# Two ScalarE functions and one refinement in place of an integer guess with three: the reciprocal roots of a layer's results in a two-layer graph network

## What is computed

```python
def _layernorm(x, axis=-1, eps=1e-05):
    m = jnp.mean(x, axis=axis, keepdims=True)
    v = jnp.var(x, axis=axis, keepdims=True)
    return (x - m) / jnp.sqrt(v + eps)

h = jnp.maximum(_layernorm(x), 0.0)
# first layer: attention over each node's edges, 4 heads of 32
alpha = einsum(q[dst], k[src]) / sqrt(32)
ea = exp(alpha - segment_max(alpha, dst)[dst])
out = segment_sum(v[src] * ea / segment_sum(ea)[dst]) + h @ Wskip + bskip
x = x + out
h = jnp.maximum(_layernorm(x), 0.0)
# second layer: messages with edge features, scaled by in-degree, summed by node
x = x + second_layer(h, src, dst, edge_attr_64)
```

## Time and profile before

| | us |
|---|---|
| median of 3 runs | 1663.34 (1662.32 to 1664.62) |
| the profiled execution's own time | 1664.58 |
| its span, first to last instruction | 1662.8 |
| TensorE busy | 1470.4 (88%) |
| VectorE busy | 1347.6 (81%) |
| ScalarE busy | 1016.5 (61%) |
| GpSimd busy | 1083.1 (65%) |

### The profile page before, as it was taken

One profiled execution on the slowest core, in us unless ns is written; L12 is line 12 of the kernel. 1 busy time (PEld: TensorE's weight loads), 2 busy tenths in 40 slices (PEclk: granted clock), 3 DMA queues, 4 the chain that ended last, 5 costly groups with the idle time before them and its releaser, 6 DMA issues. The chain is left out here.

```text
span 1662.8 us, 34477 instructions
## 1 busy us (share of the span) xinstructions
PE 1470.4 (88%) x10545; PEld 1263.5 (76%) x10546; DVE 1347.6 (81%) x3688; ACT 1016.5 (61%) x2501; POOL 1083.1 (65%) x1202
## 2 busy tenths in 40 slices
PE   5888898699999999999999974899998999998996
PEld 4666777688888888888888863777776777777775
DVE  8879665299999999999999994677776777777675
ACT  5777888556555565656665513566665666665663
POOL 2554442577777777777777605777777777777772
PEclk9999999899999999999999996999999999999999
DMA  8899887556666666666666516677666767667672
GB/s 219 274 274 313 284 300 262 157 160 180 189 174 192 175 188 183 178 182 182 182 174 185 156 45 148 148 160 174 162 163 150 171 160 172 161 158 170 149 164 68
DMA packets 162552, 302.85 MB, mean 182 GB/s; under 512 B 104113, under 2 KB 107703, under 8 KB 157524
## 3 DMA queue, kind: packets, MB, share of 16 engines
q1 hardware_dynamic: 121503, 201.19, 41.9%
q0 software_dynamic: 40896, 99.90, 24.9%
HBM read 196.84 MB, written 104.12 MB: 181 GB/s over the span
## 5 line engine op out<-in xcount | busy, mean ns | idle before, releaser
L803 POOL DMA_INDIRECT sb_kv<-kv_rows,sb_src_all x500 | 492.9, 986 | 187.1 <-issue 131.3
L831 POOL DMA_INDIRECT sb_kv<-x_rows,sb_src_all x500 | 473.8, 948 | 209.3 <-issue 109.1
L1710 ACT ACTIVATE sb_hn<-sb_xn 100x128 f32<-100x128 f32 x500 | 240.5, 481 | 265.9 <-DMA sb_kv<-x_rows,sb_src_all 225.1
L1713 ACT ACTIVATE sb_vw<-sb_kv 128x128 f32<-128x128 f32 x500 | 239.6, 479 | 0.0
L1638 ACT ACTIVATE sb_hn<-sb_xn,sb_nstat 100x128 f32<-100x128 f32 x500 | 231.5, 495 | 0.0
L1400 DVE COPY sb_hT<-ps_b 128x400 f32<-128x400 f32 x250 | 142.2, 569 | 96.1 <-PE ps_b L2005 95.3
L1797 PE MATMUL ps_b<-sb_w,sb_memberT 128*125 128x256 f32 x800 | 201.6, 391 | 18.3 <-DVE sb_xn L921 9.2
L1660 ACT COPY sb_memberT<-ps_b 100x512 f32<-100x512 f32 x150 | 75.8, 506 | 205.7 <-PE ps_b L1885 205.7
L1797 PEld LDWEIGHTS ps_b<-sb_w,sb_memberT 128*125 128x125 f32 x800 | 146.2, 193 | 41.7 <-issue 14.7
L2005 PE MATMUL ps_b<-sb_member,sb_vw 128*128 128x100 f32 x1000 | 173.8, 278 | 0.0
L2005 PEld LDWEIGHTS ps_b<-sb_member,sb_vw 128*128 128x128 f32 x1000 | 157.4, 198 | 9.8 <-issue 9.8
(11 more groups left out here) (184 smaller groups left out, 3103.0 us busy)
## 6 DMA issues: line engine op xcount, KB each, us to landing
kv_rows<-sb_kv SPq DMA_DIRECT2D x26, 1120.0 KB
sb_xn<-x_rows SPq DMA_DIRECT2D x50, 507.8 KB
sb_xn<-in_x SPq DMA_DIRECT2D x50, 500.0 KB
out_rows<-sb_xo SPq DMA_DIRECT2D x49, 500.0 KB
x_rows<-sb_xo SPq DMA_DIRECT2D x24, 1015.6 KB
sb_kv<-in_edge_attr SPq DMA_DIRECT2D x500, 32.0 KB
sb_kv<-in_x SPq DMA_DIRECT2D x28, 560.0 KB
kv_rows<-sb_xn SPq DMA_DIRECT2D x13, 1120.0 KB
```

The lines of the kernel that those rows point to most:

```text
L803: pool.indirect_dma_start(out=kvs[:, k % 4, t, :], out_offset=None, in_=kv_rows, in_offset=bass.IndirectOffsetOnAxis(ap=src_all[:, n:n + 1 ...
L831: pool.indirect_dma_start(out=xs1[:, k % 4, t, :], out_offset=None, in_=x1, in_offset=bass.IndirectOffsetOnAxis(ap=src_all[:, n:n + 1], ax ...
L1710: nc.scalar.activation(hn1[:, t, :], xn1[:, k % 4, t, 0:D], ACT.Relu, scale=xn1[:, k % 4, t, D:D + 1], bias=xn1[:, k % 4, t, D + 1:XW]).th ...
L1713: nc.scalar.activation(hs1[:, t, :], xs1[:, k % 4, t, 0:D], ACT.Relu, scale=xs1[:, k % 4, t, D:D + 1], bias=xs1[:, k % 4, t, D + 1:XW]).th ...
```

## The change

In each of the 25 sets the integer guess and two of the three refinements go. The set on VectorE now has 7 steps and 10 instructions. Its first three steps give the variance, as before. Then ScalarE computes Ln of the variance and Exp of -0.5 times that (`roots`), which is 1/sqrt, each signalling; VectorE's step 3 waits for the second of them, and steps 3 to 5 refine the value once; step 6 is the shift. ScalarE does `roots` in the turn right after `exps(k - 1)`, and so ahead of `copy_q(k + 1, 0)`. On VectorE the remaining steps stand in other places: step 3, which waits, stands ahead of `soft_step` 5 (`tot_e`), step 4 ahead of `rtot`, step 5 ahead of `wr`, step 6 behind `wr`. The statistics of the table stage keep their three refinements.

```diff
@@ -42,6 +42,7 @@
 RSQRT_BITS = float(0x5F3759DF)
 NEWTON = 3
 STAT_STEPS = 4 + 3 * NEWTON + 1
+X1_STEPS = 7
 EARLY = 2
 POOL_STEPS = 6
 NEVER = 2.0 * TILES
@@ -209,6 +210,8 @@
         var = sb("var", [128, 2 * B])
         guess = sb("guess", [128, 2, 2 * B], I32)
         nwt = sb("nwt", [128, 2, 2 * B])
+        log_var = sb("log_var", [NODES, 2 * B])
+        root = sb("root", [NODES, 2 * B])
         nstat = sb("nstat", [NODES, TILES, 2])
         pstat = sb("pstat", [ROWS, PB * B, 2])
         pool_st = sb("pool_st", [ROWS, 6, 2 * B])
@@ -402,6 +405,7 @@
                 self.aT = s("alpha_turned")
                 self.soft = s("softmax_step")
                 self.exp = s("exp_done")
+                self.root = s("reciprocal_root_step")
                 self.wT = s("weights_turned")
                 self.vw = s("values_weighed")
                 self.agg = s("agg_ready")
@@ -599,7 +603,7 @@
                 sp.dma_start(segk[:, k % 2, :], rows).then_inc(A.seg[k % 2], 16)
 
             def store(m):
-                sp.wait_ge(A.stat, STAT_STEPS * (m + 1))
+                sp.wait_ge(A.stat, X1_STEPS * (m + 1))
                 rows = x1[2 * GROUP * m:2 * GROUP * (m + 1), :].rearrange("(s p t) c -> p s (t c)", s=2, t=B)
                 slots = slice(2 * (m % 2), 2 * (m % 2) + 2)
                 from_xo = xo[:, slots, :, :].rearrange("n s t c -> n s (t c)")
@@ -1260,7 +1264,7 @@
                 m = k // 2
                 dve.wait_ge(A.xo, 3 * k + g + 1)
                 if g == 0:
-                    wait(dve, A.stat, STAT_STEPS * (m - 2) + 1)
+                    wait(dve, A.stat, X1_STEPS * (m - 2) + 1)
                     if m < 2:
                         dve.wait_ge(P.pool_stat, POOL_STEPS * (PAIRS - EARLY))
                 for t in range(first, last):
@@ -1271,11 +1275,24 @@
             def x1_stat_step(m, n):
                 if n == 0:
                     dve.wait_ge(A.bn, 2 * (m + 1))
-                wait(dve, A.stat, STAT_STEPS * m + n)
+                if n == 3:
+                    dve.wait_ge(A.root, 2 * (m + 1))
+                else:
+                    wait(dve, A.stat, X1_STEPS * m + n)
                 both = xo[:, 2 * (m % 2):2 * (m % 2) + 2, :, :]
-                stat_math(n, st[0:NODES, m % 2, :, :], both[:, :, :, D].rearrange("n s t -> n (s t)"),
-                          both[:, :, :, D + 1].rearrange("n s t -> n (s t)"), slice(0, 2 * B), NODES
-                          ).then_inc(A.stat, 1)
+                rstd, shift = (both[:, :, :, D + i].rearrange("n s t -> n (s t)") for i in range(2))
+                square, part, v = nwt[0:NODES, 0, :], nwt[0:NODES, 1, :], var[0:NODES, :]
+                if n < 3:
+                    ins = stat_math(n, st[0:NODES, m % 2, :, :], rstd, shift, slice(0, 2 * B), NODES)
+                elif n == 3:
+                    ins = dve.tensor_tensor(square, root[:], root[:], ALU.mult)
+                elif n == 4:
+                    ins = dve.scalar_tensor_tensor(part, square, -0.5, v, ALU.mult, ALU.mult)
+                elif n == 5:
+                    ins = dve.scalar_tensor_tensor(rstd, part, 1.5, root[:], ALU.add, ALU.mult)
+                else:
+                    ins = stat_math(STAT_STEPS - 1, None, rstd, shift, slice(0, 2 * B), NODES)
+                ins.then_inc(A.stat, 1)
 
             def step0(k):
                 this, prev, nxt = real(k), real(k - 1), real(k + 1)
@@ -1298,37 +1315,30 @@
                 stats(2)
                 if prev:
                     soft_step(k - 1, 1)
+                if prev:
+                    soft_step(k - 1, 2)
+                if nxt:
+                    members(k + 1, 0)
+                if prev:
+                    soft_step(k - 1, 3)
+                if prev:
+                    soft_step(k - 1, 4)
                 stats(3)
                 if prev:
-                    soft_step(k - 1, 2)
+                    soft_step(k - 1, 5)
                 stats(4)
-                if nxt:
-                    members(k + 1, 0)
+                if prev:
+                    soft_step(k - 1, 6)
                 stats(5)
                 if prev:
-                    soft_step(k - 1, 3)
+                    soft_step(k - 1, 7)
                 stats(6)
-                if prev:
-                    soft_step(k - 1, 4)
-                stats(7)
-                if prev:
-                    soft_step(k - 1, 5)
-                stats(8)
-                if prev:
-                    soft_step(k - 1, 6)
-                stats(9)
-                if prev:
-                    soft_step(k - 1, 7)
-                stats(10)
                 if this:
                     scores(k, 2)
-                stats(11)
                 if prev:
                     weigh(k - 1)
-                stats(12)
                 if this:
                     head_sums(k)
-                stats(13)
                 if nxt:
                     members(k + 1, 1)
                 if prev:
@@ -1348,31 +1358,31 @@
 
                 scores(k, 0)
                 scores(k, 1)
+                stats(0)
+                stats(1)
+                stats(2)
                 for n in range(N_SOFT):
                     soft_step(k - 1, n)
                 scores(k, 2)
-                stats(0)
                 weigh(k - 1)
-                stats(1)
                 head_sums(k)
                 for n in range(N_SOFT):
-                    stats(n + 2)
+                    if n + 3 < X1_STEPS:
+                        stats(n + 3)
                     soft_step(k, n)
                 finish(k - 1, 0)
                 finish(k - 1, 1)
                 weigh(k)
                 finish(k - 1, 2)
-                for n in range(10, STAT_STEPS):
-                    stats(n)
-                    if n < 13:
-                        x1_stats(k - 1, n - 10)
+                for g in range(3):
+                    x1_stats(k - 1, g)
                 finish(k, 0)
                 finish(k, 1)
                 x1_stats(k, 0)
                 x1_stats(k, 1)
                 finish(k, 2)
                 x1_stats(k, 2)
-                for n in range(STAT_STEPS):
+                for n in range(X1_STEPS):
                     x1_stat_step(m, n)
 
             for k in range(-1, BATCHES - 1):
@@ -1665,6 +1675,12 @@
                 act.wait_ge(A.soft, N_SOFT * k + 3)
                 nc.scalar.activation(er[:], dl[:], ACT.Exp, scale=SCALE).then_inc(A.exp, 1)
 
+            def roots(m):
+                act.wait_ge(A.stat, X1_STEPS * m + 3)
+                nc.scalar.activation(log_var[:], var[0:NODES, :], ACT.Ln).then_inc(A.root, 1)
+                act.wait_ge(A.root, 2 * m + 1)
+                nc.scalar.activation(root[:], log_var[:], ACT.Exp, scale=-0.5).then_inc(A.root, 1)
+
             def relus(k, first, last):
                 for t in range(first, last):
                     if real(k):
@@ -1678,6 +1694,8 @@
                 relus(k + 2, 0, 1)
                 if real(k - 1):
                     exps(k - 1)
+                if k % 2 == 1 and 0 <= (k - 3) // 2 < BATCHES // 2:
+                    roots((k - 3) // 2)
                 if nxt:
                     copy_q(k + 1, 0)
                 relus(k + 2, 1, 3)
@@ -1699,6 +1717,7 @@
 
             for k in range(-2, BATCHES + 1):
                 step0(k)
+            roots(BATCHES // 2 - 1)
 
             def relu1(k, t):
                 if t == 0:
```

## The result

The changed kernel takes **1725.88 us** (median of 4 runs, 1723.76 to 1728.07), the kernel before 1663.98 beside it. The ratio is 1.0369, with a 95% interval of 1.0343 to 1.0394: 62 us slower. The forecast was 1705.5, in a range of 1688 to 1754.

What follows compares the result with a forecast made beforehand. VectorE was taken to bound the attention stage. A 2.22 us wait less 0.39 saved, times 23 turns, added 42.1 to 1664.58; less 1.2 for the profiled run gave 1705.5 us, own range 1691 to 1719, stated 1688 to 1754.

Steps and rivals of the forecast that it cites:

- rival 3: Waits in each turn halve TensorE's clock, `skip` doubles: 2.0 us a turn, 46 us in all, 1751 us; chance 8%.
- Two loads a set: On ScalarE, Ln needs another table and the Exp behind it the first again: 50 loads of 1.28 us.
- Rival 2: Each table load has a tail before its ACTIVATE, up to 1.6 us: 1780 us, or 1769 by the page's drain; chance 12%.
- The wait: In each turn VectorE's step 3, due at 4.04 us, waits 2.22 us for ScalarE's root, signalled at 6.26.
- TensorE's own delay: `copy_q` comes 3.04 us later, letting `turn_weights` go at 631.1; hidden under the root's wait with 0.5 us to spare.
- The saving: Fewer VectorE instructions make a turn 0.39 us shorter before any wait for ScalarE, 0.3 to 0.5 in range.
- From `tot_e` to `wr`: Stretch of VectorE's turn holding steps 4 and 5: 1.33 us forecast, the middle between 1.41 now and 1.23 plain.
- From `wr` to the second `members`: Stretch of VectorE's turn where step 6 hides under `weigh`'s wait: 3.58 us forecast, as in a plain step, against 3.70.
- The net of an undisturbed turn: Wait minus saving in each turn, 2.22 - 0.39 = 1.83 us more, times 23 is 42.1 us.
- The last steps: Sets 23 and 24, at the end of the attention stage: a loss of 0.26 us and a gain of 0.3 cancel.
- the last chain: Set 24, variance to shift, which all wait for: 2.63 us instead of 2.37, or 1.35 without reloads.
- set 23: Its root is ready long before VectorE asks and seven instructions go: a gain set at 0.3 us, from 0 to 1.2.

Runs made afterwards that it cites:

- experiment 1: The changed kernel with the program itself loading one table for both functions, so none is placed later: 1654.85 us, ratio 0.9926 to the kernel before.
- experiment 3: The kernel before with ScalarE's Ln and Exp and their loads added, result unused and not waited for by VectorE: 1707.76 us, ratio 1.0240.
- experiment 6: The changed kernel, two loads a set, with Ln and Exp behind `copy_q` in ScalarE's order instead of ahead of it: 1747.43 us, ratio 1.0492.
- experiment 5: The changed kernel with one load a set instead of two, the table with both functions loaded ahead of each Ln: 1677.21 us, ratio 1.0059.

## Why the prediction was right, and where it was not

The forecast was 41.5 us more; 62 were measured. The chain that it followed, two loads a set, VectorE's wait for the root and a small saving, is there and accounts for 39 us (23 turns at 1.70). The rest lies outside the forecast's own sum: 17 us are TensorE's clock, some 2 us each are the first gather and the last steps. The time fell inside the stated range because that range had been stretched to take in rival 3, not because the sum was right.

- **Two loads a set: right.** The trace shows 50 rows of 1.283 us, and with one load in the whole run the same program takes 1655 us. By the Trainium skill (ScalarE: Activation LUTs, "Table sets: the hidden batching unit") a set with both functions makes it one load. The set exists, as experiment 1 shows, but it is not what was loaded here where the program said nothing.
- **A load has no tail: right.** Ln starts 0.01 us after its load has ended (620.95 + 1.28 to 622.24), and so does Exp. The drain of about 1380 ns that the Trainium skill gives on the same page ("What ACT_TABLE_LOAD costs") does not show: in 49 of the 50 the ACTIVATE starts 0.01 us behind the load, and in the 50th it waits for the variance. Rival 2 falls.
- **The wait: right.** 2.17 us for 2.22, with TensorE's own delay under it as worked out: `turn_weights` comes 0.34 behind `wr` (625.35 to 625.69).
- **The saving: a little low.** 0.39 was forecast. A pair saves 0.5 to 0.6 with one table. Two terms of the sum were too long. From `tot_e` to `wr` it takes 1.23 us (1.33 in the sum), so step 4 costs nothing there; before the change this stretch took 1.40 in the first 12 turns and 1.23 in the others, so the first 12 save 0.17 there and the others nothing. From `wr` to the second `members` it takes 3.44 (3.58 in the sum, 3.70 before), because the sum took the length of a plain step, in which `weigh` waits 0.16 for TensorE and starts 0.78 behind `wr`; in the turn it starts 0.65 behind it without a wait. The turn with one table:

```profile
628.55 0.28 DVE L1239 TENSOR_TENSOR sb_wr<-sb_er,sb_rtot 40x128 f32<-40x128 f32 x1
...
631.99 0.77 DVE L1185 TENSOR_TENSOR sb_member<-sb_drel_all,sb_iota 128x600 f32<-128x600 f32 x1
```

- **The net of an undisturbed turn: right in size.** 1.70 for 1.83. VectorE's busy time fell by 12 us and not by the 27 that I named: what went had overlapped its neighbours, and busy time counts an overlap once.
- **The clock: the step that failed.** I had it as rival 3, at 8%, with a price of 2.0 us in every turn, and summed as if it came in none. It came in 13 of 23 turns at 1.33 us, 17 us in all, which carries the time past the forecast's own range (1691 to 1719). That the new waits are shorter than the old one and split was no ground against it: two waits of 1.7 and 0.4 us with 0.75 of work between them were enough in more than half of the turns. The price was below 2.0 because the clock came back before `skip` was over: in the turn shown its second eight matmuls took 1.31 us, not 1.9.
- **The last steps: the last chain right, the rest not.** The sum had nothing for them; they cost 2.0 us. From the variance to the shift it is 2.65 us (2.63 forecast, 2.37 before), and 1.38 with one table (1.35 forecast). VectorE at the end of the changed kernel and with one table:

```profile
1056.42 0.18 DVE L869 TENSOR_TENSOR sb_var<-sb_sd,sb_sv 100x20 f32<-100x20 f32 x1
1058.41 0.18 DVE L1288 TENSOR_TENSOR sb_nwt<-sb_root 100x20 f32<-100x20 f32 x1 [1.81 <-ACT sb_root L1682]
...
1059.07 0.20 DVE L875 SCALAR_TENSOR_TENSOR sb_xo<-sb_ssum,sb_xo 100x20 f32<-100x20 f32 x1
```

```profile
992.64 0.18 DVE L869 TENSOR_TENSOR sb_var<-sb_sd,sb_sv 100x20 f32<-100x20 f32 x1
993.36 0.18 DVE L1288 TENSOR_TENSOR sb_nwt<-sb_root 100x20 f32<-100x20 f32 x1 [0.54 <-ACT sb_root L1684]
...
994.02 0.20 DVE L875 SCALAR_TENSOR_TENSOR sb_xo<-sb_ssum,sb_xo 100x20 f32<-100x20 f32 x1
```

  For set 23 I took a gain of 0.3. Its first three steps now stand in a row ahead of `fmax` with nothing to hide them, and the step in front of the last `fmax` but one takes 13.92 us where it took 13.09. A third piece comes behind the last `fmax`: TensorE has by then waited 4.73 us for `wr` in place of 3.89, its clock comes back later, and `weigh`, which stands behind its matmuls, starts 6.83 us after the last `fmax` (1047.62 - 1040.79) where it started 5.92 after it (988.66 - 982.74). TensorE and `weigh` in the changed kernel, and then in the kernel before:

```profile
1035.78 0.32 PE L1927 MATMUL ps_b<-sb_ident,sb_wr 40*128 40x40 f32 x1 [4.73 <-DVE sb_wr L1239]
...
1045.60 1.06 PE L1941 MATMUL ps_b<-sb_w,sb_hT 128*100 128x128 f32 x4
...
1047.62 1.49 DVE L1245 TENSOR_TENSOR sb_vw<-sb_kv,ps_b 128x1280 f32<-128x1280 f32 x1 [1.66 <-PE ps_b L1949]
```

```profile
987.51 0.60 PE L1922 MATMUL ps_b<-sb_w,sb_hT 128*100 128x128 f32 x4
...
988.66 1.49 DVE L1241 TENSOR_TENSOR sb_vw<-sb_kv,ps_b 128x1280 f32<-128x1280 f32 x1 [0.75 <-PE ps_b L1930]
```

  With one table the same two pieces are there (13.92, and 6.90 from the last `fmax` to `weigh`), so they don't come from the loads; what both kernels share is the new order of the steps.

In the sum from the first `fmax` to the last, 59.3 of the 59.6 us lie in the 23 pairs: 9 pairs at 1.70 are 15.3, 12 at 3.03 are 36.3, the first has 3.8, for a gather that came late, and the last, which has the lower clock and the step of 13.92, has 3.9. Why the first gather is late by another amount in each kernel was not tried.

What stays open is why the clock falls in one turn and not in the next, when the two waits are 1.67 or 1.68 and 0.41 or 0.42 us in all 13 turns in which it fell and in 8 of the 9 others (the ninth had 0.52).

## What to carry to other kernels

Before moving a function to an engine that reads functions from tables, count the table loads that it brings, one there and one back, and name what waits behind them; load a table that holds all functions in use, once, or put the loads where that engine waits anyway. Price instructions on a packed engine by distances between starts: 1.07 us of busy time a set were worth 0.5 to 0.6. And where a wait is put into an engine's way, ask what each other engine does meanwhile: here TensorE, idle for 2 us in two pieces, came back at half its clock in more than half of the turns, and each of these lost 1.3 us on top of the 1.7 that the wait had cost.

## What was not expected of the hardware

- TensorE's granted clock fell to 0.50 after waits of 1.68 and 0.42 us in 13 of 23 turns, after 1.67 us alone in 8 of 23 (experiment 3), after a single 2.85 in 20 of 23 (experiment 6), and in none with a wait of 0.39 and one of 0.42 (experiment 5).
- Constant transposes into unused columns, 14 in 1.69 us, kept the clock up in the turns, and the kernel with them is 1% faster than the changed one.
- An ACT_TABLE_LOAD took 1283 ns in each of 51 cases, and in the 26 of experiment 5, whether it went to a new table, back to the last or (experiment 5) to the one already loaded.
